# Distance projections in three rounded products, with their weights prepared in the stages before

## The reference, cut to what matters

```python
# layer 3, xn = layernorm(x)
q = heads(xn @ wq.T + bq); k = heads(xn @ wk.T + bk); v = heads(xn @ wv.T + bv)   # 16 heads of 16
q2 = sum(q * q, -1); k2 = sum(k * k, -1)
d2 = maximum(q2[..., :, None] + k2[..., None, :] - 2 * einsum('bhid,bhjd->bhij', q, k), 1e-12)
out = softmax(-sqrt(d2)) @ v;  s = out @ wo.T + bo
# gate: x_prev is x shifted by one token
xr = mu_r * x + (1 - mu_r) * x_prev;  xk = mu_k * x + (1 - mu_k) * x_prev
g = silu(sigmoid(xr @ W_r.T) * (square(relu(xk @ W_k.T)) @ W_v.T));  x = x + s * g
```

## Time and profile before

| | us |
|---|---|
| median of 3 runs | 3970.89 (3970.86 to 3974.11) |
| the profiled execution's span, first to last instruction (its own time beside it is not recorded) | 3970.3 |
| TensorE / VectorE / ScalarE / GpSimd busy in the span | 3344.4 / 3172.7 / 2284.0 / 1655.3 |
| experts' FFN, from 2556; scatter, from 2922.5; projections' stage, from 3022.4; attention, from 3272 | 365 / 98 / 250 / 698 |
| mean granted TensorE clock in the whole span | 0.911 |

### The profile page before, as it was taken

The page is one execution under the profiler, slowest core; times in us unless marked ns, Lnnn a source line. Parts: engine busy times, 40 slices in busy tenths (PEclk is TensorE's granted clock), DMA queues, the critical chain, the costliest instruction groups (busy, mean ns, idle before and its releaser), DMA issues. The chain is left out here.

```text
span 3970.3 us, 57136 instructions
## 1 busy us (share of the span) xinstructions
PE 3344.4 (84%) x16610; PEld 1749.5 (44%) x16610; DVE 3172.7 (80%) x5113; ACT 2284.0 (58%) x2725; POOL 1655.3 (42%) x773
## 2 busy tenths in 40 slices
PE   6858898888879997869799998899986987877776
PEld 3322333333337765645333343699974551112111
DVE  6869999999978887847588985577774768888887
ACT  4767666666642326624266665222212658999998
POOL 0009998989961110022100000000024337998996
PEclk9879999999989998978699999999987997788888
DMA  3553233333213347838522331211013562343442
GB/s 122 203 197 126 116 123 126 138 139 139 102 56 109 112 141 180 198 112 262 164 70 74 80 74 46 85 43 53 32 59 108 153 177 81 113 128 113 128 118 91
DMA packets 294391, 465.44 MB, mean 117 GB/s; under 512 B 40711, under 2 KB 237961, under 8 KB 273791
## 3 DMA queue, kind: packets, MB, share of 16 engines
q1 hardware_dynamic: 249838, 412.98, 32.3%
q10 hardware_dynamic: 44432, 51.10, 4.7%
HBM read 322.44 MB, written 141.33 MB: 117 GB/s over the span
## 5 line engine op out<-in xcount | busy, mean ns | idle before, releaser
L1112 PE MATMUL mamba_psum<-mamba_hc,scan_ident 128*128 128x512 f32 x1024 | 547.7, 642 | 91.2 <-DVE mamba_hc L1020 73.1
L3478 POOL TENSOR_TENSOR distance_dist<-distance_dist,distance_least_all 128x2048 f32<-128x2048 f32 x124 | 559.1, 4540 | 74.8 <-DMA distance_least_all<-distance_least_rows 74.8
L2953 POOL TENSOR_TENSOR scatter_out<-scatter_out,scatter_s 128x512 f32<-128x512 f32 x16 | 28.1, 1768 | 1026.9 <-ACT scatter_out L2969 1005.7
L1043 DVE TENSOR_TENSOR_SCAN mamba_psum<-mamba_psum,mamba_drive 128x512 f32<-128x512 f32 x352 | 414.9, 1216 | 23.1 <-issue 10.8
L2543 DVE TENSOR_REDUCE causal_row_max<-causal_psum 128x1 f32<-128x512 f32 x512 | 333.1, 683 | 79.6 <-PE causal_psum L2613 70.0
L1112 PEld LDWEIGHTS mamba_psum<-mamba_hc,scan_ident 128*128 128x128 f32 x1024 | 175.7, 195 | 418.3 <-DVE mamba_hc L1020 254.8
L2502 ACT ACTIVATE causal_probs<-causal_psum 128x1024 f32<-128x1024 f32 x256 | 250.8, 1021 | 123.7 <-PE causal_psum L2636 123.5
L3654 PE MATMUL distance_psum<-distance_shared_k_stacks,distance_shared_q_stacks 102*128 102x512 bf16 x512 | 209.9, 507 | 111.4 <-DVE distance_least L3572 55.4
L3572 DVE TENSOR_REDUCE distance_least<-distance_psum 128x2 f32<-128x1024 f32 x256 | 294.2, 1213 | 8.2 <-PE distance_psum L3654 8.1
L3608 DVE TENSOR_SCALAR distance_dist<-distance_psum 128x1024 f32<-128x1024 f32 x192 | 227.0, 1220 | 80.4 <-PE distance_psum L3669 80.4
L963 POOL TENSOR_TENSOR mamba_drive<-scan_u,scan_b_all 128x1024 f32<-128x1024 f32 x64 | 149.7, 2353 | 289.3 <-POOLq L31 289.3
(11 more groups left out here) (459 smaller groups left out, 8707.3 us busy)
## 6 DMA issues: line engine op xcount, KB each, us to landing
distance_least_all<-distance_least_rows SPq DMA_DIRECT2D x32, 1024.0 KB, 4.6
scan_b_all<-bc SPq DMA_DIRECT2D x16, 1024.0 KB
scan_c_all<-bc SPq DMA_DIRECT2D x16, 1024.0 KB, 6.3
mamba_b_all<-bc SPq DMA_DIRECT2D x16, 1024.0 KB
mamba_c_all<-bc SPq DMA_DIRECT2D x16, 1024.0 KB, 7.3
choice_w<-L_ffn_w SPq DMA_DIRECT2D x16, 1024.0 KB, 5.1
z<-mamba_in_z SPq DMA_DIRECT2D x8, 1024.0 KB, 3.9
xc<-mamba_in_xc SPq DMA_DIRECT2D x8, 1024.0 KB, 4.4
```

The lines of the kernel that those rows point to most:

```text
L1043: dve.tensor_tensor_scan(out, bank, drive[:, n % DRIVES], 0.0, ALU.mult, ALU.add).then_inc(h_ready, 1)
L1112: pe.matmul(ps[:, Y_BANK + m % 2], ident[:, :], hc[:, n % PRODUCTS], start=False, stop=(s == DS - 1)).then_inc(y_summed, 1)
L3478: pool.tensor_tensor(dist[:, g % 2, kt], dist[:, g % 2, kt], least_all[:, g % 2], ALU.subtract).then_inc(shifted, 1)
```

## The change

Three things, in one edit:

1. The weights' loads, turns and bias loads move out of `stage_distance_in` into a new class `DistanceWeights`. SP issues the loads in `experts_ffn` behind the loads of expert 1; TensorE and ScalarE turn and copy the blocks at the head of `experts_scatter`, in banks 4 to 7 (wk is scaled by -2 there). The rows lie in memory that the gather has left (`choice.late`), the identity is the experts' own, and x of batch 0 is loaded into `choice.w1` in the scatter's last round. The experts' tensors therefore live on to the end of the program, and their exit moves there.
2. q, k and v are made by `three_passes` from rounded parts of the turned x and of w_t (ScalarE rounds, VectorE subtracts).
3. `DirectSplit` takes the high part on ScalarE and the rest on VectorE straight from PSUM, without `full`; the squares are taken from PSUM too, behind each high part. Each of the four squares tiles goes to a column group of its own (32 rows of bank 4), and the norms are split as one 128-row tile over ScalarE, VectorE and GpSimd. The norms are stored by 4 transfers instead of 2.

```diff
+class DirectSplit:                      # TILES = 4, STORES = 12, sp(), pool(), act_middle() as in Split
+    def bank_free(self, eng, b, n):
+        eng.wait_ge(self.rest_ready, b * self.TILES + n + 1)
+    def act_high(self, act, b, n, bank, bias=None):
+        if n == 0:
+            act.wait_ge(self.stored, (b + 1) * self.STORES * DMA)
...
+            act.activation(self.parts[:, n, 0], bank, ACT.Identity, bias=bias).then_inc(self.high, 1)
+    def dve(self, dve, b, n, bank, bias=None):
+        dve.wait_ge(self.high, b * self.TILES + n + 1)
+        dve.wait_ge(self.ready, b * self.TILES + n + 1)
...
+            dve.scalar_tensor_tensor(self.rest[:, n], bank, bias, self.parts[:, n, 0], ALU.add, ALU.subtract).then_inc(
+class DistanceWeights:
+    def pe(self, pe, ps):
+        pe.wait_ge(self.loaded, self.LOADS * DMA)
+        for n, (src, _, _) in enumerate(self.pairs):     # 28 blocks
+            if n >= 4:
+                pe.wait_ge(self.copied, n - 3)
+            pe.transpose(ps[:, self.FIRST_BANK + n % 4, 0:P], src, self.ident[:, :]).then_inc(self.turned, 1)
 def experts_ffn      # SP
+                load_next(0)
+                distance.load(sp, nc)
+                with sp.Fori(1, NE2 - 1) as e:
+                    load_next(e)
 def experts_scatter  # heads of ScalarE's and TensorE's lists; SP, last round
+                distance.act(act, ps)
+                distance.pe(pe, ps)
+                        distance.load_x(sp, x_out, 0)
 def stage_distance_in
 # ScalarE: turn_copies, qk_copies, norms
+                        act.copy(xn_parts.high[:, m], ps[:, m]).then_inc(xn_parts.rounded, 1)
                         act.copy(xn_t[:, m, 1:], ps[:, m]).then_inc(xt_copied, 1)
-                        split.act(act, b, n, ps[:, 2 + n], bias=bias[:, side, m:m + 1], scale=1.0 if side == 0 else -2.0)
+                        split.act_high(act, b, n, ps[:, 2 + n], bias[:, side, m:m + 1])
+                        act.activation(squares[:, n], ps[:, 2 + n], ACT.Square, bias=bias[:, side, m:m + 1]).then_inc(squared, 1)
+                    act.copy(norm_parts[:, 0], ps[:, 4]).then_inc(norm_high, 1)
+                    act.wait_ge(norm_rest_ready, b + 2)
+                    act.copy(norm_parts[:, 1], norm_rest[:, :]).then_inc(norm_middle, 1)
 # VectorE
+                    if more:
+                        take_low(b + 1)
+                    dve.wait_ge(norm_high, b + 1)
+                    dve.tensor_tensor(norm_rest[:, :], ps[:, 4], norm_parts[:, 0], ALU.subtract).then_inc(norm_rest_ready, 1)
 # TensorE
-                    pe.wait_ge(norm_copied, b * 2 + 2)
+                    pe.wait_ge(norm_rest_ready, b + 1)
-                            last = pe.matmul(ps[:, 2 + n], w_t[:, Q + side, m, n2 * P:(n2 + 1) * P], xn_t[:, m, 1:], start=(m == 0),
+                            last = three_passes(pe, ps[:, 2 + n], w_parts.both((slice(None), Q + side, m, slice(n2 * P, (n2 + 1) * P))),
+                                                xn_parts.both((slice(None), m)), m == 0, m == DT - 1)
-                        pe.wait_ge(split.copied, b * split.TILES + j + 1 + split.TILES)
+                        split.bank_free(pe, b, j)
+                    split.bank_free(pe, b, split.TILES - 1)
+                    pe.wait_ge(squared, (b + 1) * split.TILES)
+                    for n in range(split.TILES):
+                        last = pe.matmul(ps[n * QUAD:(n + 1) * QUAD, 4], head_of[:, n // DT], squares[:, n], start=True, stop=True)
 # GpSimd, behind the batch's low parts
+                    pool.tensor_tensor(norm_parts[:, 2], norm_rest[:, :], norm_parts[:, 1], ALU.subtract).then_inc(norm_ready, 1)
```

More of the change, by code:

```diff
@@ L2931, in _, with pair @@
             def _(sp):
-                with sp.Fori(0, NB // 2) as i:
+                def pair(i):
                     for r in range(2):
@@ L2939, in _ @@
                         sp.dma_start(token_tiles(x_out, i * 2 + r), out[:, r]).then_inc(stored[r], DMA)
+                with sp.Fori(0, NB // 2 - 1) as i:
+                    pair(i)
+                pair(NB // 2 - 1)
                 for r in range(2):
@@ L3189, in body @@
                     split.act_middle(act, b)
-                    for n in range(split.TILES):
-                        act.wait_ge(split.copied, b * split.TILES + n + 1 + split.TILES)
-                        act.activation(squares[:, n], split.full[:, n], ACT.Square).then_inc(squared, 1)
                     if more:
@@ L3208, in _ @@
                 turn_copies(0)
+                act.copy(w_parts.high[:, :, :, :], w_t[:, 0:V + 1]).then_inc(w_parts.rounded, 1)
+                act.wait_ge(filled, FILLS)
                 batches(act, body)
@@ L3238, in norm_x, with take_low @@
                     ln.dve(dve, b, x)
+                def take_low(b):
+                    for m in range(DT):
+                        dve.wait_ge(xt_copied, b * DT + m + 1)
+                        xn_parts.take_low(dve, xn_t[:, m, 1:], (slice(None), m), b * DT + m + 1)
                 def body(b, more):
@@ L3254, in body @@
                     for n in range(split.TILES):
-                        split.dve(dve, b, n)
+                        side, m = divmod(n, DT)
+                        dve.wait_ge(squared, b * split.TILES + n + 1)
+                        split.dve(dve, b, n, ps[:, 2 + n], bias[:, side, m:m + 1])
                     dve.wait_ge(v_stored, b * DMA + DMA)
@@ L3283, in _ @@
                 norm_x(0)
+                step(dve.memset(xn_t[:, :, 0:1], 0.0))
+                step(dve.tensor_scalar(mu_not[:, :, :], mu[:, :, :], -1.0, 1.0, ALU.mult, ALU.add))
+                step(dve.tensor_scalar(bias[:, 1], bias[:, 1], -2.0, None, ALU.mult))
+                take_low(0)
+                w_parts.take_low(dve, w_t[:, 0:V + 1], (slice(None), slice(None)), 1)
+                step(dve.memset(v[:, :, :, :], 0.0))
+                step(dve.memset(v[:, :, :, HD:HD + 1], 1.0))
+                assert count[0] == FILLS
                 batches(dve, body)
@@ L3334, in body @@
                         turn(b + 1)
-                    for side in range(2):
-                        pe.wait_ge(squared, b * 2 * DT + (side + 1) * DT)
-                        pe.wait_ge(split.copied, b * split.TILES + DT + side + 1 + split.TILES)
-                        for m in range(DT):
-                            last = pe.matmul(ps[0:NH, 4 + side], head_of[:, m], squares[:, side * DT + m], start=(m == 0),
-                                             stop=(m == DT - 1))
-                        last.then_inc(norm_done, 1)
+                    split.bank_free(pe, b, split.TILES - 1)
+                    pe.wait_ge(squared, (b + 1) * split.TILES)
+                    for n in range(split.TILES):
+                        last = pe.matmul(ps[n * QUAD:(n + 1) * QUAD, 4], head_of[:, n // DT], squares[:, n], start=True, stop=True)
+                    last.then_inc(norm_done, 1)
                     pe.wait_ge(act_k_ready, b * DT + DT)
@@ L3351, in _ @@
                 turn(0)
+                pe.wait_ge(w_parts.ready, 1)
+                pe.wait_ge(made, MADE)
                 batches(pe, body)
```

241 lines of the change are left out of this document (135 added, 106 removed).

## The result

| | median, us | runs |
|---|---|---|
| before | 3970.88 | 4, 3968.32 to 3974.11 |
| after | 3939.66 | 4, 3936.18 to 3941.69 |
| forecast | 3930.9 | range 3911 to 3948 |

The change makes the kernel faster: after/before is 0.9918, with a 95% interval from 0.9904 to 0.9932. The gain is 31.2 us where 40.0 were forecast. The profiled execution of after took 3938.66 us, its span 3937.0 us.

A forecast was written before the change was run, and what follows sets the result against it. TensorE was taken to pace the projections at 25.93 us a batch, the part stores afterwards at 22.3. Gains of 23.7 (stage), 14.0 (preparation) and 2.6 (scatter) less 0.3 made 40.0: 3970.9 to 3930.9 us, range 3911 to 3948.

The forecast's parts named there:

- TensorE's part: Distance projections: TensorE's work per batch falls from 25.93 to about 21.0 us through q/k, v, squares and a removed stall.
- Loop (b): Projections: ScalarE's first operation waits for the previous batch's 12 part stores; this loop sets the batch at 22.3 us.
- Chain (a): Projections: TensorE's products, then ScalarE's queue and VectorE's subtraction, for which the next q product waits; 21.7 us per batch.
- Batches 4 and 5: Projections: SP's first attention loads delay the parts' stores and ScalarE waits; +5.5 us in all (bounds 0 and 14).
- rival 3: Projections: TensorE's waits drop its clock to 1.2 GHz for good, stage 160 us longer, 4090 us; chance 0.04.
- The last batch: Projections' last batch to the next stage's first instruction: 34.9 us becomes 31.5, SP's stores being last; gain 3.4.
- The stage: All eight batches of the distance projections together: gain 23.7 us (bounds 10 and 33).
- Preparation, 14.0 us: Before the first q product: weight loads and turns leave the path, GpSimd's memsets delay VectorE; gain 14.0 (bounds 11, 18.8).
- The scatter, 2.6 us: Start of the scatter: the weights' turns warm TensorE, so its first batch avoids half clock; gain 2.6 (bounds -1, 2.7).
- Rival 2: Projections: the part stores are the pace at 24.5 us a batch, 13 us worse, 3944 us; chance 0.15.
- Rival 1: Projections: stores land in time (issue 7.8 us), batches take 21.7 us, 12 us better, 3919 us; chance 0.16.
- Rival 4: Projections: rounded products or column groups don't pay; TensorE 23.5 us, 1.2 us per batch over forecast, 3940 us; chance 0.06.

The follow-up runs named there:

- stores_by_part: Changed kernel with one store semaphore per part, high parts stored first, each writer waiting only for its own part's stores: 3925.33 us (0.9896 of before).
- all_three: Changed kernel with stores and waits by part, the norm wait before the third product, and GpSimd's memsets after the first layer norm: 3922.09 us (0.9883 of before).
- norm_wait_late: Changed kernel with TensorE's wait for the norms' subtraction moved from the first to the third q, k product: 3935.27 us (0.9917 of before).
- the repeat: The changed kernel measured again without edits: 3937.28 us (0.9924 of before).
- fp32_products: Changed kernel with q, k, v as plain fp32 products again, rounded parts still made but unused: 3947.40 us (0.9943 of before).

## Why the prediction was right, and which terms were off

The direction, the time (8.8 us off, inside the range) and nearly every sign held. By its own steps:

- **TensorE's part.** q 5.6, v 2.9 and squares 1.1 us: measured 8.45 for q and v, 1.07 for the squares. Right; with the stall gone TensorE has 21.3 us of work in a batch (21.0 forecast). The gain of the squares is read from the rows; no run took them back alone.
- **Loop (b), 22.3 us.** The forecast took its batch time from here, and the mechanism is right: ScalarE's first operation of a batch ends its wait on the last k store. Its terms in batches 1 to 3: 10.25 us from ScalarE's first operation to the first store (10.9 forecast), 9.3 for the 12 issues (7.9), 3.2 to 4.2 for landing (3.5), in sum 22.8 to 23.7, which is what batches 2 to 4 took. The term that was mis-sized is the issue. The earlier trace rows had 9.2 us for a full batch, the prediction quoted it and took 7.9; with 9.2 its own sum would have been 23.6.
- **Chain (a), 21.7 us.** Here the path was wrong, and the changed kernel hides it under (b). I started it at TensorE's products and left VectorE out, having written that it stays under 18 us of work; it has 18.7 in batch 3, 2.7 of them the mixes' stretch. The loop goes norm copy, VectorE's subtraction, ffn, mixes, second halves, statistics, then ScalarE's Sqrt and all behind it. With the stores out of the way it is 22.53 us (stores_by_part, all_three), and taking away 1.0 us of VectorE's part gave 21.53, adding 0.33 gave 22.86.
- **Batches 4 and 5.** The parts of batch 4 held ScalarE 2.9 us longer, as I had it (3): they began 1.4 us later and the last took 5.7 us to land instead of 3.3, while their issue took 0.9 less. What I had not carried on is what follows: after TensorE's 3.80 us wait the clock was 0.50 for some 6 us, and batch 5 took 28.73 instead of 25.3. It is rival 3's mechanism, in one batch and not for good. That the clock is the cause of the last 3 us is read from the rows and was not tested alone; norm_wait_late, with a shorter stretch at 0.50 and a batch shorter by as much, bears it out. With the wait gone (stores_by_part) the batch is normal.
- **The last batch.** 32.8 us instead of 31.5: four norm stores took 4.4 us to issue, not 2.2, and the parts 8.3, not 7.8; from the last norm store to the next stage it was 4.0 us, not 4.9.
- **The stage**: 17.4 us where 23.7 were forecast. The missing 6.3 are 3.4 in batches 1 to 4, 2.1 in 5 and 6, 1.3 in the last, less 0.4 gained in the first.
- **Preparation, 14.0 us.** Measured 12.7 to 12.8. The memsets held three of the four layer norm operations, not two: the first took 0.41 us, the others 1.97 each. Without the memsets the preparation takes 12.9 us, 4.5 less (4.8 forecast).
- **The scatter, 2.6 us.** Right for its first batch against two of the three profiles of before (19.2 us to the second rounding, now 16.6; the third has 18.0). At the end 1.1 us are left on the means, and likely most of the 2.6 like against like.
- **The clock and the turns.** Turns bring up the clock: 0.74 over them, 1.00 right behind, as the row of before had said. In the nine profiles with the turns at the scatter's head the clock comes back to 1.00 at 4.7 to 7.4 us after the FFN's last VectorE operation, in the four without them at 11.7 to 14.4 us. The Trainium skill ("TensorE: Matmul & The Clock Gate", Part 4: PE-mode transpose) says that the full clock doesn't engage for transposes. These fp32 turns don't bear that out.
- **Exits.** +0.9 at the end and -0.5 in the middle: +0.4 in all, where I had +0.3.
- **What was left at nothing**, the 19 loads in the FFN and the attention: nothing, within a variation of 11.5 and 5.6 us.

Rival 2 (the stores are the pace, 3944) had the place right and its time is nearer than the forecast's (4.3 us off; against the repeat both are off by about as much), though its 24.5 us a batch are too many: what filled the gap was the issue and batch 5's clock. Rival 1's issue of 7.8 us did not come in batches 1 to 3. Rival 3 did not come for the stage, whose mean clock is 0.95; two of its numbers were wrong: 0.88 is a stretch of 2 us and the scatter's mean is 0.84, and 80 of 236 us at half speed make a mean of about 0.83, not 0.78. Rival 4 is refuted by the changed kernel's rows (8.45 and 1.07 us). What the rounded products are worth is told by fp32_products: 8 to 10 us of the 31.

## What to carry to other kernels

When the engine that sets the pace is relieved by 5 us, list every loop over the other engines with its real stretched durations before naming the new bound; a busy total under the batch time proves nothing, since a loop is a sum over engines. A wait placed in front of the first operation of a batch holds all that its engine does: make it one wait per buffer. Keep GpSimd away from VectorE's fast one-input operations, and its tensor_tensors from VectorE's two-input ones too, and test a moved operation at its new place, where it may hold another kind.

## What the runs showed of the hardware

- Four 128x512 tensor_scalars took 1.67 us alone and 4.40 beside GpSimd tensor_tensors; four scalar_tensor_tensors with two SBUF operands took 2.73 beside none and 5.79 beside them. Beside memsets of GpSimd, four 128x256 tensor_scalars took 6.09 instead of 1.38, and two-input tensor_tensors were not stretched (0.69 us each).
- It goes both ways: a GpSimd product of 128x1024 took 5.12 us when it began just before VectorE's two-input operations (the kernel before), and 2.68 beside the one-input ones that it held.
- TensorE's wait for the rests was followed by a stretch at clock 0.50 when it was 3.36 to 4.43 us long (batch 5 of five profiles; the stretch was about 7 us long, in norm_wait_late half that). One of 2.28 us (batch 6 of fp32_products) was followed by such a stretch too, one of 2.26 us (norm_wait_late) was not, and none of 0.66 to 1.79 us was.
- The same stretch ahead of the stage, in which only 19 loads were added, varies by 11.5 us between executions (2911.2 to 2922.7 in thirteen profiles). A difference of 4 us between two profiles in such a stretch is no effect.
